# Slot attention inside a decoder kernel: scores without a normed query, update sums in six banks, chunk by chunk alternation on TensorE

## What is computed

```python
Pn = rmsnorm(P, input_norm_w)
k_proj = jnp.einsum('bmd,ed->bme', Pn, Wk)
v_proj = jnp.einsum('bmd,ed->bme', Pn, Wv)
for _ in range(NUM_ITERS):
    sn = rmsnorm(slots, slot_norm_w)
    q = jnp.einsum('bkd,ed->bke', sn, Wq)
    scores = jnp.einsum('bkd,bmd->bkm', q, k_proj) * scale
    attn = jax.nn.softmax(scores, axis=-2)
    attn = attn / (jnp.sum(attn, axis=-1, keepdims=True) + EPS)
    updates = jnp.einsum('bkm,bmd->bkd', attn, v_proj)
    slots = gru_cell(updates, slots, gru_wi, gru_wh, gru_bi, gru_bh)
```

## Time and profile before

| | us |
|---|---|
| median of 3 runs | 1482.36 |
| lowest and highest run | 1465.57, 1485.68 |
| span of the profiled execution | 1480.7 |
| head block, to the start of `prepare_context` | 270.6 |
| `prepare_context`, to the first score matmul | 54.2 |
| three iterations, first score matmul to routing | 756.6 |
| routing, experts, combine | 399.3 |

### The profile page before, as it was taken

One profiled execution on the slowest core, in us unless ns is written; L12 is line 12 of the kernel. 1 busy time (PEld: TensorE's weight loads), 2 busy tenths in 40 slices (PEclk: granted clock), 3 DMA queues, 4 the chain that ended last, 5 costly groups with the idle time before them and its releaser, 6 DMA issues. The chain is left out here.

```text
span 1480.7 us, 20506 instructions
## 1 busy us (share of the span) xinstructions
PE 1278.3 (86%) x6518; PEld 1042.5 (70%) x6518; DVE 978.8 (66%) x2065; ACT 626.2 (42%) x1057; POOL 294.6 (20%) x369
## 2 busy tenths in 40 slices
PE   3898789668999997999999799999953999999960
PEld 3456678436777775777777577777743999999960
DVE  4325775566886575788656578865676677777747
ACT  4112322243444332444433233443341677777744
POOL 5704100120000000000000000000002566666633
PEclk9999999688999999999999799999975899999995
DMA  5000000500000000000000000005073111111134
GB/s 190 1 0 1 0 30 15 167 1 0 1 1 0 1 1 1 1 0 1 1 0 1 1 1 0 1 1 227 1 258 116 37 43 46 43 45 40 50 107 142
DMA packets 39720, 58.21 MB, mean 39 GB/s; under 512 B 4637, under 2 KB 33246, under 8 KB 39262
## 3 DMA queue, kind: packets, MB, share of 16 engines
q1 hardware_dynamic: 32958, 42.40, 8.4%
q0 software_dynamic: 4416, 12.06, 2.6%
q10 hardware_dynamic: 2272, 2.81, 0.5%
HBM read 44.94 MB, written 12.32 MB: 39 GB/s over the span
## 5 line engine op out<-in xcount | busy, mean ns | idle before, releaser
L75 PE MATMUL x_psum<-x_sn_lo,x_kq_hi 128*128 128x512 f32 (+1 forms) x312 | 134.9, 432 | 30.7 <-issue 9.4
L655 POOL TENSOR_TENSOR x_E_rest<-x_E_rest 128x512 f32<-128x512 f32 x12 | 15.5, 1290 | 725.7 <-ACT x_E_rest L649 725.7
L75 PE MATMUL x_psum<-x_p_lo,x_v_hi 128*128 128x512 f32 (+1 forms) x312 | 130.6, 419 | 6.7 <-ACT x_E_rest L789 4.8
L867 DVE TENSOR_REDUCE x_mx<-x_psum 128x1 f32<-128x512 f32 (+1 forms) x156 | 104.4, 687 | 40.3 <-PE x_psum L77 40.0
L76 PE MATMUL x_psum<-x_sn_hi,x_kq_lo 128*128 128x512 f32 (+1 forms) x312 | 128.5, 412 | 0.0
L77 PE MATMUL x_psum<-x_sn_hi,x_kq_hi 128*128 128x512 f32 (+1 forms) x312 | 128.3, 411 | 0.0
L76 PE MATMUL x_psum<-x_p_hi,x_v_lo 128*128 128x512 f32 (+1 forms) x312 | 125.7, 403 | 0.0
L77 PE MATMUL x_psum<-x_p_hi,x_v_hi 128*128 128x512 f32 (+1 forms) x312 | 125.5, 402 | 0.0
L789 ACT ACTIVATE x_e<-x_psum,x_inv,x_rs 128x1024 f32<-128x1024 f32 (+1 forms) x39 | 47.1, 1207 | 180.4 <-DVE x_inv L874 180.4
L75 PE MATMUL e_bank<-e_w_lo,e_g_hi 128*128 128x256 f32 x368 | 107.7, 293 | 0.1
L75 PE MATMUL e_bank<-e_xT_lo,e_w_hi 128*128 128x256 f32 x368 | 105.6, 287 | 1.4 <-DVE e_xT_lo L1707 1.4
(11 more groups left out here) (373 smaller groups left out, 3391.2 us busy)
## 6 DMA issues: line engine op xcount, KB each, us to landing
w<-in_w SPq DMA_DIRECT2D x16, 1024.0 KB, 12.0
w<-scratch_results SPq DMA_DIRECT2D x8, 512.0 KB, 7.6
a_x<-in_x SPq DMA_DIRECT2D x1, 2048.0 KB, 12.7
sT<-in_xT ACTq DMA_DIRECT2D x1, 2048.0 KB, 11.4
scratch_x<-a_h SPq DMA_DIRECT2D x4, 512.0 KB, 2.9
r_x<-scratch_x SPq DMA_DIRECT2D x4, 512.0 KB, 5.4
scratch_x<-r_x SPq DMA_DIRECT2D x1, 2048.0 KB, 12.3
w<-scratch_x SPq DMA_DIRECT2D x1, 2048.0 KB, 8.5
```

The costliest lines, as they stand in the source:

```text
L75: pe.matmul(out, w_hi, x_lo, start=start, stop=False)
L655: pool.tensor_tensor(sq[:, 0], sq[:, 0], sq[:, 1], ALU.add).then_inc(sum_ok, 1)
L867: mark = k.mark(v.tensor_reduce(mx[0:n, m % 2, c:c + 1], bank[c][0:n], AX_X, ALU.max))
```

## The change

The cross attention is written anew. Around it nothing changes but the place of some tiles and the freeing of the head's semaphores. What is different:

- The three iterations are unrolled.
- Scores are taken of the slots as they are (`x_s_hi`, `x_s_lo`). The slot norm is a row `x_rsb`, broadcast over partitions, that DVE multiplies in when it reads scores from PSUM: one `tensor_tensor_reduce` (scale_scores, L831) gives scaled scores in SBUF and the maximum. It replaces L867. For chunks 0 to 2 the row goes through DRAM: a 16-byte store of each partition and a broadcast load by SyncE (spread_rs); for chunk 3 it is still one diagonal and one fp32 matmul.
- Scores use only banks 0 and 1 in turn (the first eight scores have more). Banks 2 to 7 hold update sums of chunks 0 to 2, six banks. TensorE alternates: score of (m, c), then update of (m - 2, c). Chunk 3's weights are kept (`E3`) and updated in a tail of 13 updates.
- ACT takes exponentials in place in SBUF (1536 + 512 columns), scales them in place (1536 + 512), and copies three high parts of 512. DVE's low parts are plain subtractions of 512 columns (L843).
- The sum `x_acc` moves from DVE to POOL (L954: 1536 + 512 columns for each tile).
- Partition sums use all of `ones` as the moving side, so 128 columns in place of 1 (L713 for squares, L1015 for rows). The inverse row sums go through DRAM, one store and four broadcast loads, in place of the four L1008 broadcasts.
- GRU: order hn, r, in, z; norm work in halves of 512; the update of the next chunk is split at h = 1, ahead of DVE's chain for that h.

The diff, cut to its core:

```diff
-                    for c in range(NC):
-                        if m == 0 and c == 1:
-                            norm.normed(v, it * NC + NC - 1, NC - 1)
-                        if m == 0 and c == 2:
-                            norm.normed_lo(v, it * NC + NC - 1, NC - 1)
-                        v.wait_ge(score_mm, it * MT * NC + m * NC + c + 1)
-                        mark = k.mark(v.tensor_reduce(mx[0:n, m % 2, c:c + 1], bank[c][0:n], AX_X, ALU.max))
-                        if c == 0 and m >= 1:
-                            weights_lo(m - 1)
...
+                    v.tensor_tensor_reduce(out, bank[score_bank(i)][0:n], rsb[0:n, chunk(c)], rs16[0:n, m:m + 1], -3.0e38,
+                                           ALU.mult, ALU.max, mx[0:n, m % 2, c:c + 1]).then_inc(scaled, 1)
...
+                scale_scores(0)
+                rms(v, k, it, LAST)
+                for i in range(1, 8):
+                    scale_scores(i)
+                negated(0)
+                inverse(0)
+                negated(1)
+                inverse(1)
+                for c in range(KEEP):
+                    weights_lo(c, 0, c, c)
+                for m in range(2, MT):
+                    for c in range(NC):
+                        scale_scores(place_of[(m, c)])
+                    negated(m)
+                    for c in range(KEEP):
+                        weights_lo((m - 1) * KEEP + c, m - 1, c, ((m - 1) % 2) * KEEP + c)
+                    inverse(m)
+                for c in range(KEEP):
+                    weights_lo((MT - 1) * KEEP + c, MT - 1, c, ((MT - 1) % 2) * KEEP + c)
+                for m in range(MT):
+                    weights_lo(MT * KEEP + m, m, LAST, TAIL_SLOTS[m % 4])
...
+                    act.activation(e[0:n, m % 2], e[0:n, m % 2], ACT.Exp, bias=inv[0:n, m, 0:1],
+                                   accum_out=mx[0:n, m % 2, NC:NC + 1]).then_inc(exp_ok, 1)
+                    act.activation(E3[0:n, m], E3[0:n, m], ACT.Exp, bias=inv[0:n, m, 0:1],
+                                   accum_out=mx[0:n, m % 2, NC + 1:NC + 2]).then_inc(exp_ok, 1)
+                    act.wait_ge(inv_ok, it * MT + m + 1)
+                    act.activation(e[0:n, m % 2], e[0:n, m % 2], ACT.Copy, scale=inv[0:n, m, 2:3]).then_inc(p32_ok, 1)
+                    act.activation(E3[0:n, m], E3[0:n, m], ACT.Copy, scale=inv[0:n, m, 2:3]).then_inc(p32_ok, 1)
...
+                            pool.wait_ge(acc_ok, (it * MT + m - 1) * 2 + part + 1)
+                            pool.tensor_tensor(to, to, src, ALU.add).then_inc(acc_ok, 1)
...
+                for i in range(3):
+                    score(i)
+                square_sums(pe, it, LAST)
+                score(3)
+                score(4)
+                pe.wait_ge(diag_ok, it + 1)
+                pe.matmul(bank[6], ones[:], diag[:], start=True, stop=True).then_inc(bc_mm, 1)
+                for i in range(5, 8):
+                    score(i)
+                for m in range(2, MT + 2):
+                    for c in range(NC):
+                        if m < MT:
+                            score(place_of[(m, c)])
+                        if c == LAST:
+                            continue
...
+                        update((m - 2) * KEEP + c, m - 2, c, ((m - 2) % 2) * KEEP + c)
...
+                        if h == 1 and c + 1 < NC:
+                            updates_lo(c + 1)
+                        if h == 1 and c >= 1 and more:
+                            rms(v, k, it + 1, c - 1)
```

More of the change, by code:

```diff
@@ L1 @@
+import math
 from contextlib import ExitStack
@@ new lines, in _ @@
+                for m in range(MT):
+                    weights_lo(MT * KEEP + m, m, LAST, TAIL_SLOTS[m % 4])
+                    if m == 7:
+                        v.wait_ge(row_mm, it + 1)
+                        k.step(v.tensor_scalar(rw[:, 0], bank[2][:, 0:8 * NT].rearrange("p (t n) -> p t n", t=NT)[:, :, 0], EPS_RMS, None, ALU.add))
+                        v.reciprocal(rw[:, 1], rw[:, 0]).then_inc(row_ok, 1)
+                normed(0)
+                updates_lo(0)
+                normed(1)
@@ new lines, in score @@
+                    if frees(i) is not None:
+                        pe.wait_ge(scaled, it * NS + frees(i) + 1)
+                    elif it >= 1 and b in (0, 1, 7):
+                        pe.wait_ge(mult_ok, it * NC)
+                    elif it >= 1:
+                        pe.wait_ge({2: hr_ok, 3: r_ok, 4: arg_ok, 5: z_ok}[b], it * GH)
+                    for h in range(DH):
+                        pe.wait_ge(s_lo_ok, it * GH + c * DH + h + 1)
+                        last = three_pass(pe, bank[b][0:n], kq_hi[:, h, ks], kq_lo[:, h, ks],
+                                          s_hi[:, h, chunk(c)], s_lo[:, h, chunk(c)], h == 0, h == DH - 1)
@@ new lines, in score, with update @@
+                    last.then_inc(score_mm, 1)
+                def update(j, m, c, slot):
+                    n = MROWS[m]
+                    pe.wait_ge(p_lo_ok, it * NP + j + 1)
+                    for h in range(DH):
+                        b = 2 + DH * c + h if c < KEEP else h
+                        last = three_pass(pe, bank[b], v_hi[0:n, m, hs(h)], v_lo[0:n, m, hs(h)],
+                                          p_hi[0:n, slot], p_lo[0:n, slot], m == 0, m == MT - 1)
+                    last.then_inc(upd_mm, 1)
@@ L1026, in gate @@
+                    updates = [(wi_hi, wi_lo, u_part(p_hi, c)[:, k], u_part(p_lo, c)[:, k], k) for k in range(DH)]
                     steps = slots * ("s" in parts) + updates * ("u" in parts)
                     for i, (w_hi, w_lo, x_hi, x_lo, k) in enumerate(steps):
-                        if x_hi is updates[0][2]:
+                        if "u" in parts and i == len(steps) - DH:
                             pe.wait_ge(u_lo_ok, it * NC + c + 1)
@@ L1226, in _ @@
                 last.then_inc(wkq_mm, 1)
-            norm.broadcast(pe, 0, 0)
-            norm.square_sums(pe, 2, 2)
+            first["square_sums"](pe, 0, 0)
             pe.wait_ge(wkq_ok, DH)
```

783 lines of the change are left out of this document (370 added, 413 removed).

## The result

The changed kernel took 1500.22 us (median of 4 runs, 1496.82 to 1501.28), the kernel before 1473.96 (4 runs, 1456.13 to 1485.68). The ratio is 1.0289 with a 95% interval from 1.022 to 1.0358: slower. The forecast was 1489 with a range from 1458 to 1520, and "within 2%" as the likeliest case (0.63). The time lies in the range, but what came is the case that had 0.23: slower by over 2%. The executions of the kernel before spread far more than the changed one's (1447 to 1486 over all comparisons here), and the profile of before is one of its longer ones, so spans are compared with its span, 1480.7, and the ratio is read with care. The profiled execution of the changed kernel has a span of 1498.7 us: 18.0 more.

A forecast was written before the change was run, and what follows sets the result against it. TensorE, busy 86% of the span, was taken as the bound. Iterations of 256.2, 254.2 and 250.5 make 760.9 against 756.6, +4.3; prepare_context +2.5; span 1487.5, with 1.7 some 1489 us; range 1458 to 1520.

The forecast's parts named there:

- the case that had 0.23: Whole kernel: slower by over 2%, above 1512.0 us, made up of rivals A and B; chance 0.23.
- 14.7: Behind the last score: waits of 2.1 and 4.2 us for low parts, and twice three updates of 4.2 us.
- GRU: GRU stage: 288 matmuls 67.2, twelve square sums 3.6, hn waits of 1.45 at two chunks; 73.7 us.
- 13 x 1.4 and 16 row sums: Tail of the score stage: 18.2 us of updates plus 4.8 of row sums, 23.0 us.
- Rival A: TensorE's partition sums: 128-column sums cost 0.72 us each, as in the head; +41 us, 1530; chance 0.10.
- The first wait: Iteration's beginning: TensorE waits 10.9 us for DVE's first low part, ends 5 and 15; then 2.0 us lost to lower clock.
- the 16.5: Iteration's beginning: TensorE reaches the first update 16.5 us after the first score starts.
- The steady tile: Score stage's middle: 9.8 us of matmuls plus a 0.7 us wait for x_p_lo, 10.5 us; pair 0.93 us.
- Rival B: Score stage: DVE's scaling pair passes the bank twice, 1.5 us; 9.4 us an iteration, +28, 1517; chance 0.13.
- rival C: Score stage: add never meets low part, pair 0.69, sum 0.24 us; 9.2 us less an iteration, 1461; chance 0.14.
- POOL's add and DVE's low part: Behind the last score: two SBUF-input instructions hold each other up; 3 us charged, ends 0 and 3.69.
- The gap at the loop's turn: Ahead of the next iteration's first score: 4.6 us goes in each iteration, since score matmuls follow the GRU directly.

The follow-up runs named there:

- the orders and ACT's moved copy together: Changed kernel: tile 0's low parts before tile 1's inverse, steady first low part before last scaling, POOL's last adds after low parts, ACT's copy later; span 1462.5 us.
- the four costs: Changed kernel, each undone alone: spread stationary sides (wrong slots) 1478.3, steady low part's order 1484.1, first low parts' order 1489.5, POOL's last add 1489.9 us span.
- The last kernel: Changed kernel plus reordered DVE/POOL work, later ACT copy and scaling, neighbouring columns for row and lead sums, inverse sums turned by matmul; median 1447.27 us, span 1444.9.

## Why the prediction was right and wrong

The mechanism forecast was a wash: what the change takes off is paid back at the two ends of the score stage, with no gain in its middle, +6.8 us of span. That is how the trace looks, with +18.0. The 11 us between them lie in the three iterations, which came out 5.0, 3.1 and 4.2 above their forecasts; the rest came out 1.1 under. Its terms for the second iteration, and what was measured (254.2 and 257.33 in all):

| term | forecast | measured |
|---|---|---|
| beginning: to the end of the first 36 matmuls of updates and scores | 37.8 | 37.4 |
| ten steady tiles | 105.0 | 102.7 |
| from the last score to the end of tile 12's updates | 14.7 | 17.4 |
| tail with row sums | 23.0 | 26.3 |
| GRU | 73.7 | 73.6 |

- **The step that was off is what stands behind the last score**, "14.7" and "13 x 1.4 and 16 row sums", 23.0: 37.7 together, 43.7 measured. Two terms were too small. The row sums cost 0.42 and not 0.3 (+2.0): I had set their price by the number of moving columns, between 0.24 and 0.72, and that number turned out to be free; the price was that of the stationary side, which the diff changed in the same line and of which the text said nothing. No run shows the 0.3: the trace of before has 0.72 in the head and 0.56 in routing, there at a clock of 0.50 (1122.00 to 1123.50), and the runs had 0.42 with the spread stationary side and 0.22 with the neighbouring one. And the matmuls behind the wait of 3.43 us ran at a clock of 0.50 to 0.52 (+4.7, of which 3.5 in tile 12's updates and 1.2 in the tail). I charged such a loss behind the first update's wait, where it was 1.4 us, and none here. The two waits themselves were 1.2 us shorter than forecast (1.64 and 3.43, not 2.1 and 4.2).
- **The nearness of the sum is in part luck.** The beginning and the ten tiles were forecast 2.7 us too high, what follows them 6.0 too low.
- **The sums' stationary side is as large as the whole loss.** With it undone, and the sums of the wrong slots, the changed kernel stands at 1478.3, level with before. It is not the only such term: the orders and ACT's moved copy together are worth 36.2. Rival A, "the 128-column sums cost 0.72", pointed at the right instruction with the wrong cause and too high a price. Its row of the head stays unexplained: those weight loads (L507) took 310 ns too, with neighbouring columns, and the trace has no record of the granted clock before 129.9 us.
- **The first wait**: 10.9 forecast, 9.44 measured, at 18.2 from the start and not 16.5, because the eight sums took 3.5 us and the broadcast waited 0.75. (The terms named for the 16.5, nine scores of 1.4, eight sums of 0.3 and a broadcast of 0.86, make only 15.9.) The stated cause, tile 1's inverse in front of tile 0's low part, is shown for 3.3 us of it by the run that changed only this; the other 6.1 are the chain of DVE and ACT that the forecast walked through, not tested by itself.
- **The steady tile**: 10.5 forecast, 10.27 measured; the pair costs 0.75 (0.67 from one to the next when they stand in a row), not 0.93. The wait was x_p_lo behind the scaling, as walked; shown by the run that moved the low part. Rival B is out. The part of rival C that asked for a pair of 0.69 came nearly true, and was worth 2.3 us of an iteration and not 4.
- **POOL's add and DVE's low part**: 3 us charged at tile 12, 3.3 measured (5.20 for three low parts and not 1.89), and shown both ways. The scaling, with one input in PSUM, stayed at 0.750 beside POOL, as L934 had at 0.744 to 0.752 before.
- **GRU** was right as a sum by two errors: its twelve sums took 5.0 us and not 3.6, its two waits 0.35 each and not 1.45.
- **The gap at the loop's turn**: I booked 4.6 us for each iteration. The kernel before, unrolled, gained 13.3 in all, but not there; a norm stood under the gap. In the changed kernel the scores do follow the GRU directly (no gap in front of 587.82), because they need no norm. That this is what un-normed scores brought is read from the two traces; no run here has one without the other.

An account from measured parts: the change gave 13.3 (unrolling, on before) and 5.5 (wide moving side, on before), and 18 broadcasts fewer at 0.86, 15.5, in all 34. Some 3 us stand in it twice, since in the unrolled kernel the clock no longer fell behind two of the three runs of sums, so 31 is nearer. It is 18.0 slower, so it paid some 49. Undoing the four costs, one by one, gave back 20.4 + 14.6 + 9.2 + 8.8 = 53.0. The last kernel gave back 53.8, but with the moved copy and ACT's later scaling as well, and with the squares of the GRU stage still spread. So the parts add up to within some 4 us; this is arithmetic of this case and not a proof, since some of them share waits and the two figures on before are of single executions of a kernel that spreads.

## What to carry to other kernels

In a chain of small matmuls read the access pattern of the stationary side as closely as its size: columns at a distance made each weight load 1.6 times as long, and 36 small sums an iteration cost as much as the whole loss. If a layout is chosen for a DMA, turn the small result with one matmul and not the large operand with a stride. And in a strict queue ask of every instruction that waits what ready work stands behind it: moving one 0.7 us instruction ahead of such a wait won 0.5 us thirty times over, more than any other change of order here.

## What was unexpected of the hardware

- A load of 128 fp32 stationary columns took 192 ns when they were neighbours (with the wrong slots) and 311 when they lay 64 bytes apart (the changed kernel), both at a granted clock of 1.00; 16 bytes apart (the squares) the median was 329 over loads at clocks of 1.00 and 0.50.
- 16 fp32 sums take the same time with 1 and with 128 moving columns (6.75 and 6.79 us), but behind the narrow ones the granted clock was 0.64 in one kernel and 0.52 in another, behind the wide ones 1.00 in both. In the unrolled kernel it was 1.00 behind two of three runs of narrow ones; why stays open.
- The clock's loss did not follow the length of the wait: 1.4 us behind a wait of 9.44, 4.7 behind one of 3.43, nothing behind 1.20 and 1.64. It followed how much of the low stretch met work: 2.9 us of it behind the first, over 10 behind the second. With the long wait cut to 6.10 us, 6.15 us of low clock stood behind it, and that iteration won 1.0 us of the 3.3. What sets the start of a low stretch is open; no run here was made for it.
- A reciprocal of 512 columns on DVE, read from PSUM: 3.35 us.
- A store of 8 KB in pieces of 4 bytes: 10.9 us, against 1.4 in pieces of 64 bytes.
